# Transposes of the attention output share the two PSUM banks of the exponentials, in one ring

## What is computed

```python
h = tok(x)                                    # Haar wavelets of a 96x96 image, 64 tokens
h = concatenate([h, txt], axis=1)             # 192 tokens of 64
h = h + attn0(layernorm(h))                   # softmax(h h^T / 8) h
h = h + ffn0(layernorm(h))                    # top half of the tokens by a router, gelu MLP
h = h + attn1(layernorm(h))                   # 16 query heads, 1 key head, rope, rmsnorm,
                                              # causal window of 128, output projection wo
h = h + ffn1(layernorm(h))                    # argmax over 32 experts, relu MLP
```

## Time and profile before

| What | Value |
|---|---|
| Median of three runs | 582.66 us (579.9 to 582.99) |
| The profiled execution, whole | 583.62 us |
| Its span on the chip | 581.8 us |
| TensorE matmul busy | 502.2 us, 86% of the span |
| VectorE busy | 417.8 us, 72% |
| ScalarE busy | 311.9 us, 54% |
| GpSimd busy | 234.7 us, 40% |

### The profile page before, as it was taken

One profiled execution on the slowest core, in us unless ns is written; L12 is line 12 of the kernel. 1 busy time (PEld: TensorE's weight loads), 2 busy tenths in 40 slices (PEclk: granted clock), 3 DMA queues, 4 the chain that ended last, 5 costly groups with the idle time before them and its releaser, 6 DMA issues.

```text
span 581.8 us, 14569 instructions
## 1 busy us (share of the span) xinstructions
PE 502.2 (86%) x5920; PEld 386.4 (66%) x5920; DVE 417.8 (72%) x1291; ACT 311.9 (54%) x593; POOL 234.7 (40%) x217
## 2 busy tenths in 40 slices
PE   3457499879999899989998999899989999899845
PEld 2235277658867786778776877688767767777622
DVE  3669766996799769976997699957995697363220
ACT  1414346565667556766577565756575655454311
POOL 2316632554446342643454436354462446420000
PEclk9999999989999999999998999899999999999966
DMA  7000000000000000000000000000000000000000
GB/s 271 1 6 0 1 7 2 3 1 7 3 2 10 7 2 2 10 7 3 2 9 3 2 3 2 8 3 2 3 10 2 2 2 9 2 3 9 2 1 7
DMA packets 6450, 6.29 MB, mean 11 GB/s; under 512 B 4208, under 2 KB 5744, under 8 KB 6256
## 3 DMA queue, kind: packets, MB, share of 16 engines
q1 hardware_dynamic: 6384, 5.37, 3.0%
HBM read 4.31 MB, written 0.79 MB: 9 GB/s over the span
## 4 chain that ended last, share of the span: by engine, by line
PE 47%; DVE 35%; ACT 9%; POOL 2%; issue 2%; DMA 2%; SPq 1%; POOLq 0%; ACTq 0%; DVEq 0%
PE bank L961 38%; PE bank L979 10%; DVE eq L515 5%; DVE negm L631 4%; DVE q_sb L568 4%; DVE ssq L585 4%; DVE tb L568 4%; DVE on L648 3%; ACT qT L810 3%; POOL qs L793 2%; DMA p<-masks 2%; DVE eq L506 1%; ACT qs L810 1%; DVE eq L431 1%; DVE rec L644 1%
## 5 line engine op out<-in xcount | busy, mean ns | idle before, releaser
L631 DVE TENSOR_REDUCE negm<-bank 128x2 f32<-128x384 f32 (+1 forms) x128 | 79.2, 619 | 39.6 <-PE bank L961 38.4
L793 POOL TENSOR_TENSOR qs<-q_sb,qs 128x1024 fp32r<-128x1024 f32 x24 | 56.8, 2368 | 107.8 <-ACT qs L810 107.8
L919 ACT ACTIVATE p<-bank 128x512 f32<-128x512 f32 x112 | 66.0, 599 | 56.6 <-PE bank L961 55.4
L961 PE MATMUL bank<-kh,qT 128*128 128x128 f32 (+1 forms) x384 | 82.0, 323 | 0.0
L810 ACT ACTIVATE qT<-bank 128x512 fp32r<-128x512 f32 x96 | 54.3, 596 | 50.3 <-PE bank L979 49.9
L961 PE MATMUL bank<-vx,p 128*64 128x65 f32 x1536 | 68.8, 225 | 1.3 <-DVE on L648 1.2
L961 PEld LDWEIGHTS bank<-vx,p 128*64 128x64 f32 x1536 | 60.5, 138 | 13.9 <-issue 6.8
L756 POOL TENSOR_TENSOR q_sb<-q_sb,tb 128x512 f32<-128x512 f32 x24 | 36.5, 1519 | 74.3 <-DVE tb L568 74.3
L961 PEld LDWEIGHTS bank<-kh,qT 128*128 128x128 f32 x384 | 64.2, 199 | 2.1
L961 PE MATMUL bank<-sh_r,sh_l 128*128 128x512 f32 x112 | 53.2, 475 | 0.0
L644 DVE RECIPROCAL rec<-bank 128x4 f32<-128x4 f32 (+1 forms) x88 | 15.7, 179 | 48.4 <-PE bank L961 48.0
(11 more groups left out here) (158 smaller groups left out, 1122.9 us busy)
## 6 DMA issues: line engine op xcount, KB each, us to landing
wts<-weights SPq DMA_DIRECT2D x1, 1313.5 KB, 7.3
h<-txt SPq DMA_DIRECT2D x1, 672.0 KB, 8.4
img<-images SPq DMA_DIRECT2D x8, 72.0 KB, 1.9
q_sb<-wqkv SPq DMA_DIRECT2D x1, 576.0 KB, 9.7
sh_r<-mT SPq DMA_DIRECT2D x32, 4.0 KB
out<-o_sb SPq DMA_DIRECT2D x8, 64.0 KB, 1.9
p<-masks SPq DMA_DIRECT2D x1, 480.0 KB, 10.4
cst<-shapes SPq DMA_DIRECT2D x1, 304.0 KB, 3.8
```

The costliest lines, as they stand in the source:

```text
L631: ve.tensor_reduce(dst, src, AX_X, ALU.max, negate=True).then_inc(s_vec, 1)
L793: gp.tensor_tensor(qs[:, :, D:2 * D], ta[:, t, 0:NH, :], qs[:, :, 0:D].bitcast(F32), ALU.subtract).then_inc(b_pool, 1)
L919: ac.activation(dst.rearrange("s h t -> s (h t)"), bank[BANK_E[n % 2]][:, :], ACT.Exp).then_inc(e_act, 1)
L961: return pe.matmul(dst, lhsT, rhs, start=start, stop=stop, skip_group_check=True)
```

## The change

The transposes X0 to X5 move from bank 7 to banks 5 and 6, where they take turns with the exponentials. The order of that ring is fixed: it is the order of E and X in `C_ORDER`, 20 entries for a pair, and an entry's place in it gives its bank. One semaphore on each side (`e_pe`, `e_act`) counts both kinds.

- V0, V4 and V8 on TensorE wait only for the scaling of the value step before them, no longer for the copy of a transpose.
- An X waits for the copy or exponential two places before it in the ring, and for the scaling that fills its half of `on`. X1, X3 and X5 no longer wait for the copy of X0, X2 and X4.
- VectorE gets three new waits. The scaling of V4 waits for the transposes X1, that of V8 for X3, and that of V0 for X5 of the pair before, because they overwrite what those read.
- `C_ORDER` changes: E5, E6 come before X0, X1; X0 and X1 are next to each other, and so are X2 and X3, which have E10 before them and E11 behind.
- All five strings of `MERGE` are new, so the order of all work on all engines is new. No instruction is added or removed.

```diff
-C_ORDER = ["E0", "E1", "V0", "E2", "V1", "E3", "V2", "E4", "V3", "X0", "E5", "X1", "V4", "E6", "V5", "wo0", "E7", "V6",
-           "E8", "V7", "X2", "E9", "X3", "E10", "E11", "wo1", "E12", "V8", "E13", "V9", "V10", "X4", "X5", "wo2"]
+C_ORDER = ["E0", "E1", "V0", "E2", "V1", "E3", "V2", "E4", "E5", "V3", "E6", "X0", "X1", "V4", "E7", "wo0", "V5", "E8", "V6",
+           "E9", "V7", "E10", "X2", "X3", "E11", "wo1", "V8", "E12", "E13", "V9", "V10", "X4", "X5", "wo2"]
+RING_E = [x for x in C_ORDER if x[0] in "EX"]
...
+                    if v in (4, 8):
+                        ve.wait_ge(e_pe, after(RING_E, p, f"X{v // 2 - 1}"))
+                    elif v == 0 and p.n > 0:
+                        ve.wait_ge(e_pe, after(RING_E, p, "X5") - len(RING_E))
...
-                    if v in (0, 4, 8):
-                        pe.wait_ge(x_act, p.n * 6 + v // 2)
-                    else:
-                        pe.wait_ge(o_vec, p.n * NV + v)
+                    pe.wait_ge(o_vec, p.n * NV + v)
...
-                    if n in (0, 2, 4):
-                        pe.wait_ge(o_vec, p.n * NV + {0: 4, 2: 8, 4: 11}[n])
-                    else:
-                        pe.wait_ge(x_act, p.n * 6 + n)
+                    pe.wait_ge(e_act, after(RING_E, p, f"X{n}"))
+                    pe.wait_ge(o_vec, p.n * NV + (4, 4, 8, 8, 11, 11)[n])
```

More of the change, by code:

```diff
@@ L128 @@
            "S": [("B", x) for x in B_ORDER if x[0] == "S" or x[:2] == "mT"],
-           "E": [("C", x) for x in C_ORDER if x[0] == "E"],
-           "V": [("C", x) for x in C_ORDER if x[0] != "E"],
+           "E": [("C", x) for x in C_ORDER if x[0] in "EX"],
+           "V": [("C", x) for x in C_ORDER if x[0] not in "EX"],
            "D": [("D", x) for x in D_ORDER]}
 MERGE = {
[33 rows of a table removed]
[32 rows of a table added]
 }
@@ L320, in early_fusion @@
         o_pe, o_rec, o_vec = sem("o_pe"), sem("o_rec"), sem("o_vec")
-        x_pe, x_act = sem("x_pe"), sem("x_act")
         d_vec, d_pool, d_pe, d_act = sem("d_vec"), sem("d_pool"), sem("d_pe"), sem("d_act")
@@ L361, in f @@
                     if pair.n > 0:
-                        sp.wait_ge(e_pe, (pair.n - 1) * 14 + (4, 8, 14)[t])
+                        sp.wait_ge(e_pe, after(RING_E, pair, ("E3", "E7", "E13")[t]) - len(RING_E))
                     if t < 2:
@@ L917, in f @@
                         ac.wait_ge(d_pe, p.n * len(D_PE))
-                    ac.wait_ge(e_pe, p.n * 14 + n + 1)
-                    ac.activation(dst.rearrange("s h t -> s (h t)"), bank[BANK_E[n % 2]][:, :], ACT.Exp).then_inc(e_act, 1)
+                    ac.wait_ge(e_pe, after(RING_E, p, f"E{n}"))
+                    ac.activation(dst.rearrange("s h t -> s (h t)"), bank[BANK_E[RING_E.index(f"E{n}") % 2]][:, :],
+                                  ACT.Exp).then_inc(e_act, 1)
                 return f
@@ L927, in f @@
                         ac.wait_ge(d_pe, after(D_PE, p, f"y{n // 2 - 1}"))
-                    ac.wait_ge(x_pe, p.n * 6 + n + 1)
-                    copy(dst.rearrange("k h t -> k (h t)"), bO[:, :]).then_inc(x_act, 1)
+                    ac.wait_ge(e_pe, after(RING_E, p, f"X{n}"))
+                    copy(dst.rearrange("k h t -> k (h t)"), bank[BANK_E[RING_E.index(f"X{n}") % 2]][:, :]).then_inc(e_act, 1)
                 return f
@@ L1159, in f @@
                             pe.wait_ge(set_pool, 4)
-                    pe.wait_ge(e_act, p.n * 14 + n + 1)
-                    b = bank[BANK_E[n % 2]][:, :]
+                    pe.wait_ge(e_act, after(RING_E, p, f"E{n}"))
+                    b = bank[BANK_E[RING_E.index(f"E{n}") % 2]][:, :]
                     if n < 8:
@@ L1184, in f @@
                     w = D + 1
-                    if v in (0, 4, 8):
-                        pe.wait_ge(x_act, p.n * 6 + v // 2)
-                    else:
-                        pe.wait_ge(o_vec, p.n * NV + v)
+                    pe.wait_ge(o_vec, p.n * NV + v)
                     if v < 8:
-                        pe.wait_ge(e_act, p.n * 14 + v + 3)
+                        pe.wait_ge(e_act, after(RING_E, p, f"E{v}") + 2)
                         for j in range(4):
@@ L1194, in f @@
                         if v < 10:
-                            pe.wait_ge(e_act, p.n * 14 + {8: 13, 9: 16}[v])
+                            pe.wait_ge(e_act, after(RING_E, p, {8: "E10", 9: "E13"}[v]) + 2)
                         lo, hi = PAIRS_OF_HEADS[v]
@@ L1209, in f @@
                 def f(p):
-                    if n in (0, 2, 4):
-                        pe.wait_ge(o_vec, p.n * NV + {0: 4, 2: 8, 4: 11}[n])
-                    else:
-                        pe.wait_ge(x_act, p.n * 6 + n)
+                    pe.wait_ge(e_act, after(RING_E, p, f"X{n}"))
+                    pe.wait_ge(o_vec, p.n * NV + (4, 4, 8, 8, 11, 11)[n])
                     srcs = [on[:, 8 * (n % 2) + 2 * j:8 * (n % 2) + 2 * j + 2, :] for j in range(4)]
-                    transposes(bO, [s.rearrange("q h d -> q (h d)") for s in srcs], ident, x_pe)
+                    transposes(bank[BANK_E[RING_E.index(f"X{n}") % 2]], [s.rearrange("q h d -> q (h d)") for s in srcs],
+                               ident, e_pe)
                 return f
@@ L1223, in f @@
                 def f(p):
-                    pe.wait_ge(x_act, p.n * 6 + 2 * t + 2)
+                    pe.wait_ge(e_act, after(RING_E, p, f"X{2 * t + 1}") + 2)
                     if t == 0:
```

## The result

| | us, median | runs between | against before |
|---|---|---|---|
| kernel before | 581.37 | 579.9 and 582.99 | |
| changed kernel | 596.99 | 596.53 and 597.4 | 1.0259 [1.0228, 1.029] |

The changed kernel is slower by 15.6 us. The forecast was 586.0 us, 3.3 more than the median it started from (582.66, three runs) and 4.6 more than this one, with a range up to 596: the sign was right, the size was not, and the time lies 1.0 us above the range. The profiled execution took 597.11 us (span 595.3).

A forecast was written before the change was run, and what follows sets the result against it. TensorE sets the pace, VectorE follows closely. From 583.62 us, +5.0 for five periods, -1.0 up to 500 and -0.75 at the end gave 586.9, or 586.0 as a median 0.96 lower; range 573.5 to 596.

The forecast's parts named there:

- the 2.6 us of a period: Middle period, X2 to X2: TensorE idle 2.6 of 60.70 us, laid to VectorE's late scaling behind rank2, not the bank.
- The freed bank gives 0.75 us: Last pair: X5 no longer waits for the copy of X4, a sure gain of 0.75 us.
- E7 pays 0.4 a period: TensorE, behind X1: E7 needs X0's copy in the ring, charged 0.4 us a period, could be 0 to 0.6.
- The stretch from S8's end to V4: TensorE waits for VectorE's late V3 scaling, ready at 26.2 us; 2.5 us of standing taken, ends 0.7 and 3.0.
- my 23.8: Time after S8's end at which TensorE's own work would let it start V4, in us.
- kk's cast is undisturbed: VectorE's keys' split: cast L618 runs free beside m0, subtraction L620 is held to m0's end; nothing charged.
- the slow rival: kk held twice, L618 by m0 and L620 by m1; kTh, E8, V6 start 1.9 us late each period: 596 us, chance 0.13.
- rank3 on lo1 costs 0.4: VectorE's rank3 meets GpSimd's lo1, so S3 waits 0.4 us for S2's maxima, range 0 to 1.5.
- all else 0.3: Small TensorE waits that stay in a period, some 0.3 us.
- Five periods at 1.0 us: Middle periods with the full mix: 61.7 against 60.70 us, 1.0 us more each, +5.0 us over five.
- -1.0 to 500: Stretch up to 500 us: part A gone, VectorE lighter by tok, ln1, xn1 and ctx; a gain of 1.0 us.
- 0 at the start: First 80 us and first transition: no change, +-2.5 us, since the first chain's order is nearly the same.

The follow-up runs named there:

- the experiment that took it away: Changed kernel with GpSimd's small norm steps, ln1 of A and ln of D, moved ahead of rot0: 601.99 us, 1.0326 against the kernel before.
- the memsets: Changed kernel and kernel before, zero-writes replacing fifteen of sixteen heads of GpSimd's low-part subtraction, step about as long: 584.06 us (1.0053) and 584.52 us (1.0033).
- The single-tile runs: Changed kernel with zero-writes replacing fifteen heads of GpSimd's low-part subtraction in one query tile only: lo0 592.81 us, lo1 594.34 us, lo2 592.54 us.

## Why the prediction was wrong, step by step

1. *TensorE sets the pace, and the 2.6 us of a period are VectorE's lateness behind rank2.* Right: moving rank2 alone gave 6.2 us against the kernel before on its chip, the ring alone gave nothing.
2. *The freed bank gives 0.75 us, E7 pays 0.4 a period.* Nearly right. The last X5 follows X4 without a gap (one row of eight transposes at 567.64), so its wait is gone, and E7 waits 0.25 us for X0's copy (437.34 in the changed kernel's timeline of TensorE). The ring's gain in the old order is not measurable. What I had not worked out is what the new order would be without the ring, 14.6 us more.
3. *The stretch from S8's end to V4: TensorE starts V4 26.2 us after S8's end.* It was 25.8 (406.80 to 432.58), and kTh came at 33.0 (439.78) against a forecast of 33.2. The total was right, its parts less so: I had TensorE standing for 2.5 us. It stood for 0.28 (S9), 0.36 (D xT), 0.23 (mT2) and 0.23 (V4); the other 0.9 us of the 2.0 by which it missed my 23.8 are in its busy time. VectorE's idle time ahead of D xT was 0.96 us against 0.8, and the experiment that took it away gained nothing: the diagnosis of the wait was right, and that it was a cost to be cured was not.
4. *kk's cast is undisturbed, its subtraction is held to the end of m0, at no charge.* Right: 0.54 and 1.47 us in the middle periods, and no wait of TensorE behind them there. So the slow rival (596 us) came near the time by luck; its mechanism did not occur.
5. *The other half of a period: rank3 on lo1 costs 0.4, all else 0.3.* This is the step that failed. From kTh to the next S8 end I had 61.7 - 33.2 = 28.5 us, and it took 30.18; beside the memsets, with the first half unchanged at 33.0, it took 27.66. So the held steps cost 2.5 us in a period, where I had charged 0.4 for rank3, and what I had counted was 0.8 us too dear in this half. My waits add up to 3.6 us and TensorE did stand for 3.65, but that is luck: I had 2.9 in the first half and 0.7 in the second, and it was 1.50 and 2.16. TensorE's own work I had at 58.1 us and it was 59.51; of that miss 0.55 goes with the held steps. I saw one of the three steps that met the subtraction. xn2 and the product y I never placed against lo0 and lo2, though the earlier trace rows had shown in rank2 and m0 what such a meeting does. The single-tile runs price them: rank3 at 2.7 us over the span, about what I had charged (0.4 in five periods), xn2 at 4.2 and y at 4.5, which I had at zero.
6. *Five periods at 1.0 us, -1.0 to 500, 0 at the start.* The middle periods cost 2.46 each instead of 1.0. From the second pair's kk to the seventh's, five periods, the changed kernel took 317.1 us and the kernel before 307.2, 9.9 more where I had 5.0. In the profile of before three of the five took 61.9 instead of 60.7 us, at a granted clock of 0.97 to 0.98; at equal clock the five would cost some 13.6. The rest, start, last pair and end, came to +3.6 us (13.5 in all by the spans, less 9.9) where I had -1.75. It was not tested apart, and its parts are not clean: in the first 80 us the changed kernel was granted a clock of 0.89 and the kernel before 1.00. With the subtraction gone from both kernels nothing of it is left in their medians, which makes holds likely there too; shown it is not.
7. *The range.* Its upper end rested on one rival, the held cast. The bound for the unplaced steps, worked out from the earlier trace rows as for rank2 (up to 2 us for each step beside each long GpSimd instruction), was missing. With it the range would have reached beyond 600. That the measured time is only 1.0 us above the range is luck: what set that end did not occur.

The Trainium skill's rule (SBUF — State Buffer, Who interferes with whom) was applied in the prediction to kk alone, where it changed nothing. It bore on every step with two inputs that the new order lays beside a subtraction, and the row of the product (2.51 us beside lo2, 0.36 beside memsets) agrees with it.

Still open: why the last pair's stretch is 8.4 us longer from kk to kk (61.7 us, against 53.3) and the first 8.6 us shorter (56.5 against 65.1). Work of neighbouring pairs has moved between them, and no run took them apart.

## What to carry to other kernels

When an order is changed, lay every VectorE step that reads two tensors from SBUF, or normalises as these do, against GpSimd's long instructions in the new order, and price each meeting at the rest of the GpSimd instruction, before counting waits. The engines' busy sums hardly show it (VectorE's rose by 1.9 us a period): VectorE had 10 us to spare in each period, and the holds still set the time, since reductions that TensorE needs stand behind them. And look at who is really late ahead of a wait for a bank: one step moved on VectorE gave more than the new banks did.

## What the runs showed of the hardware

- How long a VectorE instruction is held depends on what GpSimd does, not only on whether it is busy: beside a subtraction of 2.4 us that reads two tensors, a SCALAR_TENSOR_TENSOR of 0.42 us took 1.69 and a TENSOR_TENSOR of 0.36 took 2.51; beside memsets, which together last as long, both kept 0.42 and 0.36. The Trainium skill (SBUF — State Buffer, Who interferes with whom) says that an instruction with two SBUF inputs doesn't contend with a GpSimd one that only writes, and the rows agree.
- Three TENSOR_SCALARs with one tensor input each were held as well: 2.83 us beside the subtraction, 0.75 free, and 1.09 beside the memsets, where all three ended within 0.12 us after the first memset of 0.90 us. So writing holds them too, and that they were free so soon may be due to the shortness of that memset. The same section of the Trainium skill (SBUF — State Buffer, Who interferes with whom) says that a tensor_scalar can use both ports when its operands allow it, and then contends with GpSimd; which would explain both rows. That it used them here was not measured.
- The cast of the keys' split (128x384 from 128x384) took 0.54 us beside m0.
- The number of matmuls in a period is the same, but TensorE's busy time by the profile, whose matmul ends are modelled, went from 58.08 to 59.51 us in the new order and to 58.96 in the same order with memsets. So the gain of 2.5 us a period was 1.96 us of idle time and 0.55 of busy time: idle time alone didn't show all that the held steps cost.
